# Six PSUM banks for the opening of layer 1, roundings one pair behind the tanh, and unread products around the attention of layer 0

## The chip, the cores and the metric

The kernel runs on one core of one Trainium2 chip. The metric is the device time of one execution in microseconds (us). A measurement of this kernel is the median of a few runs.

## The reference, cut to what matters

Two transformer layers over 1024 tokens of width 256. Each layer adds an attention and a feed-forward part, both computed from the same layer norm, to its input:

```python
x = L0_attn_X                                   # (1, 1024, 256)
xn = _layernorm(x)
x = x + _L0_attn_ref(xn, ...) + _L0_ffn_ref(xn, ...)   # 16 heads of 16, rope, causal; 1024 hidden, sign weights
xn = _layernorm(x)
x = x + _L1_attn_ref(xn, ...) + _L1_ffn_ref(xn, ...)   # 16 heads, 64+64 (rope) wide keys, 128 wide values
# _L1_ffn_ref: 32 experts of width 96, the best 4 for each token, and a shared expert:
sh = jax.nn.silu(x @ shared_gate_w.T) * (x @ shared_up_w.T)       # 512 hidden
shared_gate = jax.nn.sigmoid(x @ shared_expert_gate_w.T)
out0 = shared_gate * (sh @ shared_down_w.T)
```

## The kernel before, in words

Most products are made of three: each fp32 operand is split into a rounded part ("hi", copied to fp32r by ScalarE) and the rest ("lo", a subtraction on GpSimd or VectorE), and hi·hi, lo·hi and hi·lo are added in PSUM. PSUM is one tensor `bank` of eight banks of 512 fp32 columns. Each engine's program is written out by hand; semaphores order them. Between the blocks all engines meet.

**Block 1, `project_layer0`.** Layer norm, transposition, q, k and v of layer 0 with rope, then its feed-forward part. The last of TensorE's work is the down projection, 8 tiles of 16 products (line 453).

**Block 2, `attend_layer0`.** Eight pairs of heads. TensorE's order is a sorted list of steps that have a time in units of one pair. "max" steps (12 a pair, lines 680 and 662) make the scores of one row tile of both heads in one of two double banks; VectorE takes their row maxima (line 621). The "shift" step (line 691) transposes the maxima of the pair, which SyncE then writes as two more rows of q. "exp" steps (9 a pair, lines 708 and 659) make the transposed scores, shifted by these rows; ScalarE takes their exponentials (line 603). Pair p's max steps begin `LEAD` = 1.4 pairs ahead of its exp steps. "mix" steps (line 726) multiply the exponentials with v, into bank 7 (`O_BANK`); the first is at time 1.2. VectorE takes each finished half group out of bank 7 (line 638, semaphore `taken`). The score products have 48 or 50 contracted rows for each head, the mixes 32 columns of weights.

**Block 3, `join_layer0`.** Output projection (line 832), the sum, the second layer norm, transposition and the router's logits. Its first products wait until ScalarE has rounded `wo` (line 774) and VectorE has made the rest (line 798).

**Block 4, `layer1`.** It opens with the shared expert. TensorE's work is cut into units that each fill one bank; `unit_done` and `unit_free` count them. Units 0 to 7 are four pairs (gate, up), two for each of two slices of the hidden width; 8 to 15 are four q/k projections of head 0 (`qk_unit`) in turn with four output products (`out_unit`), the first of which waits for the lo part of all four pairs; 16 to 23 are four more pairs (5 to 8). Then come v of round 0 (four units from `V0_UNIT` = 24, line 1733), scores of the first rows and four more output products. All of them use banks 6 and 7 in turn (`unit_bank`), so unit n waits for `unit_free` ≥ n − 1. Banks 0 to 3 are for scores, 4 and 5 for transpositions.

For a pair, ScalarE takes the tanh of the gate half (line 1286), VectorE makes (tanh + 1)·gate (line 1361), multiplies by the up half (line 1365) and by the token's gate (line 1368), ScalarE rounds (`hidden_hi`, line 1259) and GpSimd makes the rest (`hidden_lo`, line 1614). Two buffers `hid`, which are the tanh's too, are used in turn. ScalarE's program for a pair is: tanh, one rounding of weights, `hidden_hi` of the same pair. Between the pairs VectorE also does the routing: softmax, the best four, weights, choice, and after the fifth pair (`HALF_UNIT[1]`) `route_place`, which yields the row of each token and expert in `slot_x`. Then GpSimd scatters the tokens (line 1638): four after the lo part of pair 6, four after that of pair 7, eight after that of pair 8, then it normalises the first rows of probabilities (line 1627), which the first transposition of the rounds (line 1824) waits for. After that come eight rounds of two heads, in which the experts' tiles are interleaved.

## Time and profile before

| | |
|---|---|
| times of three runs | 993.98, 996.51, 1004.88 us |
| median | 996.51 us |
| the profiled execution's own time | 1002.6 us |
| span of its profile | 1000.8 us |
| TensorE busy | 874.6 us, 87% |
| VectorE busy | 635.3 us, 63% |
| ScalarE busy | 421.8 us, 42% |
| GpSimd busy | 343.8 us, 34% |
| mean granted TensorE clock | 0.919 of 2.4 GHz |

The span leaves out 1.8 us of the execution's time. "Busy" counts a TensorE product from its start to its modelled end. The blocks meet at 80.4 us (layer-0 attention begins), 240.0 us (join) and 272.0 us (layer 1); the rounds' first transposition is at 359.5 us.

### The profile page before, as it was taken

How to read it: one execution, taken by the hardware profiler on the slowest of the kernel's cores; microseconds unless marked ns; L12 is line 12 of the kernel's file. 1: busy time of each engine (PE TensorE's matmuls, PEld its weight loads, DVE VectorE, ACT ScalarE, POOL GpSimd, SP SyncE). 2: the span in 40 equal slices, each digit the busy share in tenths (PEclk: the TensorE clock that was granted, in tenths of full speed). 3: DMA queues.
4: the chain of work that ended last, by engine and by line, in shares of the span. 5: the costliest groups of instructions: out<-in, count | busy, mean ns of one | idle time of the engine just before them, and what ended most of it. 6: DMA issues, size and time to landing. Idle time of an engine off the chain costs nothing.

```text
span 1000.8 us, 17106 instructions
## 1 busy us (share of the span) xinstructions
PE 874.6 (87%) x5280; PEld 605.1 (60%) x5280; DVE 635.3 (63%) x1179; ACT 421.8 (42%) x959; POOL 343.8 (34%) x333
## 2 busy tenths in 40 slices
PE   3697998886777777899999999999999999999665
PEld 2584544434555665576676676676767667667444
DVE  5697658753578546557656756756666666676552
ACT  3230546674322133435534625635535544543230
POOL 2340000001043675624423424324323433435780
PEclk9896559997878788999999999999999999999778
DMA  6550222420030111404413323422432331341221
GB/s 246 197 153 27 70 71 81 120 71 23 22 117 11 63 66 40 132 22 156 131 52 121 131 79 126 130 80 89 131 115 89 128 118 52 122 150 37 59 77 55
DMA packets 52773, 94.08 MB, mean 94 GB/s; under 512 B 6980, under 2 KB 27980, under 8 KB 52460
## 3 DMA queue, kind: packets, MB, share of 16 engines
q1 hardware_dynamic: 49660, 85.16, 26.7%
q0 software_dynamic: 3072, 8.39, 2.6%
q8 instruction: 24, 0.39, 0.2%
q14 instruction: 17, 0.14, 0.0%
HBM read 75.43 MB, written 24.78 MB: 100 GB/s over the span
## 4 chain that ended last, share of the span: by engine, by line
PE 48%; DVE 3%; issue 2%; POOL 2%; ACT 1%; POOLq 0%; DVEq 0%; ACTq 0%
PE bank L1841 10%; PE bank L1761 9%; PE bank L1711 7%; PE bank L1824 5%; PE bank L1751 4%; PE bank L1865 4%; PE bank L1733 3%; PE bank L1877 2%; PE bank L1858 1%; POOL d_gathered L1648 1%; DVE d_swap L1388 1%; PE bank L1764 1%; PE bank L1874 1%; DVE d_rot L1388 1%; PE bank L1749 0%
## 5 line engine op out<-in xcount | busy, mean ns | idle before, releaser
L1627 POOL TENSOR_SCALAR d_probs<-d_probs,d_row_inv 128x1024 f32<-128x1024 f32 (+7 forms) x128 | 99.3, 780 | 191.7 <-DVE d_row_inv L1416 190.8
L1268 ACT ACTIVATE d_probs<-bank,d_neg_max 128x1024 f32<-128x1024 f32 (+7 forms) x128 | 95.9, 753 | 104.4 <-DVE d_neg_max L1411 104.1
L1841 PE MATMUL bank<-d_pT,d_v 128*128 128x512 f32 (+3 forms) x384 | 130.9, 491 | 0.4 <-ACT d_pT L1315 0.4
L1411 DVE TENSOR_REDUCE d_neg_max<-bank 128x1 f32<-128x1024 f32 (+7 forms) x128 | 95.7, 753 | 51.4 <-PE bank L1764 50.7
L1315 ACT COPY d_pT<-bank 128x512 f32<-128x512 f32 x192 | 86.2, 488 | 80.2 <-PE bank L1824 80.2
L1841 PEld LDWEIGHTS bank<-d_pT,d_v 128*128 128x128 f32 x384 | 72.8, 192 | 59.6 <-issue 47.3
L621 DVE TENSOR_REDUCE b_maxes<-bank 128x2 f32<-128x1024 f32 (+2 forms) x96 | 89.0, 949 | 29.7 <-PE bank L662 20.1
L1824 PE MATMUL bank<-ident,d_probs 128*128 128x128 f32 x576 | 88.5, 285 | 15.3 <-POOL d_probs L1627 10.4
L1761 PE MATMUL bank<-d_k_hi,d_q_hi 128*128 128x512 f32 x192 | 78.3, 408 | 18.8 <-POOL d_k_lo L1621 14.2
L603 ACT ACTIVATE b_probsT<-bank 128x512 f32<-128x512 f32 x132 | 72.2, 594 | 48.3 <-PE bank L659 37.3
L1621 POOL TENSOR_TENSOR d_q_lo<-d_rot,d_q_hi 128x512 fp32r<-128x512 f32 x32 | 40.9, 1279 | 138.1 <-ACT d_q_hi L1264 138.1
L1824 PEld LDWEIGHTS bank<-ident,d_probs 128*128 128x128 f32 x576 | 66.8, 145 | 34.2 <-POOL d_probs L1627 12.9
L1761 PE MATMUL bank<-d_k_hi,d_q_lo 128*128 128x512 f32 x192 | 68.6, 358 | 0.0
L1761 PE MATMUL bank<-d_k_lo,d_q_hi 128*128 128x512 f32 x192 | 68.3, 356 | 0.0
L584 POOL TENSOR_TENSOR heads_lo<-acc,heads_hi 128x512 fp32r<-128x512 f32 x8 | 10.2, 1276 | 160.1 <-ACT heads_hi L609 160.1
L1711 PE MATMUL bank<-xT_hi,d_qkw_hi 128*128 128x512 f32 x128 | 57.5, 449 | 8.4 <-DVE d_slot_hT L1581 4.5
L1761 PEld LDWEIGHTS bank<-d_k_hi,d_q_hi 128*128 128x128 f32 x192 | 38.1, 199 | 38.1 <-issue 17.7
L1401 DVE TENSOR_TENSOR d_rot<-d_rot,d_swap 64x512 f32<-64x512 f32 x64 | 55.7, 871 | 6.7
L1564 DVE TENSOR_TENSOR d_head_lo<-bank,d_head_hi 128x512 fp32r<-128x512 f32 x32 | 22.1, 692 | 59.5 <-ACT d_head_hi L1323 59.3
L1388 DVE TENSOR_TENSOR d_swap<-bank,d_sin 32x512 f32<-32x512 f32 x64 | 44.4, 693 | 19.1 <-PE bank L1711 17.8
L1386 DVE SCALAR_TENSOR_TENSOR d_swap<-bank,d_gs_now,d_sin 32x512 f32<-32x512 f32 x64 | 48.2, 753 | 11.2 <-PE bank L1711 9.3
L1711 PE MATMUL bank<-xT_hi,d_qkw_lo 128*128 128x512 f32 x128 | 51.6, 404 | 0.0
(276 smaller groups left out, 2019.2 us busy)
## 6 DMA issues: line engine op xcount, KB each, us to landing
d_expert_w<-in_expert_w SPq DMA_DIRECT2D x102, 320.0 KB, 3.2
d_slot_x<-slot_x SPq DMA_DIRECT2D x51, 128.0 KB, 2.9
slot_y<-d_slot_y SPq DMA_DIRECT2D x49, 128.0 KB, 3.3
qk_raw<-in_w_qk SPq DMA_DIRECT2D x16, 256.0 KB, 3.3
slot_x<-in_zeros SPq DMA_DIRECT2D x5, 768.0 KB, 5.9
slot_x<-in_zeros SPq DMA_DIRECT2D x3, 896.0 KB, 6.4
d_vw_raw<-in_w_v SPq DMA_DIRECT2D x9, 256.0 KB, 3.2
q_stack<-a_part_hi SPq DMA_DIRECT2D x4, 512.0 KB, 5.1
```

The lines of the kernel that those rows point to most:

```text
L603: nc.scalar.activation(probs(head, n), bank[:, E_BANK + t % 3, :], ACT.Exp, scale=SCALE0).then_inc(exped, 1)
L621: nc.vector.tensor_reduce(maxes[:, p % 2, c, :, i], bank[:, first:first + 2, 0:w], AX_X, ALU.max, negate=True).then_inc(maxed, 1)
L1268: nc.scalar.activation(probs[s % NP_][:, 0:width(s)], score_bank(s, width(s)), ACT.Exp, bias=neg_max[:, h.col(s)], accum_out=row_sum[:, h. ...
L1315: nc.scalar.copy(pT[c][:, j:j + blocks, col:col + P], bank[:, T_BANK + tu % 2, 0:blocks * P].rearrange("p (b q) -> p b q", b=blocks)).then ...
L1388: return nc.vector.tensor_tensor(dst, src[rows, :], table[rows, cols], ALU.mult)
L1401: nc.vector.tensor_tensor(rot[n % 2][DS:P, :], rot[n % 2][DS:P, :], swap[DS:P, :], ALU.add).then_inc(rotated, 1)
L1411: nc.vector.tensor_reduce(neg_max[:, h.col(s)], score_bank(s, width(s)), AX_X, ALU.max, negate=True).then_inc(maxed, 1)
L1627: nc.gpsimd.tensor_scalar(probs[s % NP_][:, 0:width(s)], probs[s % NP_][:, 0:width(s)], row_inv[:, h.col(s)], 1.0, ALU.mult, ALU.mult).the ...
L1711: last = nc.tensor.matmul(out, parts(a, k), b[:, k, cols], start=(k == 0 and n == 0), stop=(k == KT - 1 and n == 2))
L1761: last = nc.tensor.matmul(out, a["q"][:, rows], b["k"][:, cols], start=(n == 0), stop=(n == 2 and not diagonal))
L1824: last = nc.tensor.transpose(bank[:, T_BANK + tu % 2, b * P:(b + 1) * P], probs[n % NP_][:, (j + b) * P:(j + b + 1) * P], ident[:])
L1841: last = nc.tensor.matmul(bank_of(h, "pv", n)[:, q:CH], v[:, j, h.hh, :], pT[c][:, j, q:CH], start=(j == 0), stop=(j == len(pieces) - 1))
```

## The change

Four edits.

1. In block 1 TensorE issues 14 products of 128x128 by 512 bf16 columns behind its last work, into bank 0. They and all below multiply the constants `halves`, and nothing reads their result.
2. In block 2 TensorE's list gets steps "keep", one such product each, into bank 7: 12 between the max steps of pair 0 (times from −1.36 to −0.48), and then one every 0.05 of a pair from −0.38 to 1.12, which are 31. When the last half group has been taken (`taken` = 8), 20 more follow.
3. Units 0 to 23 of layer 1 use banks 6, 7, 0, 1, 2 and 3 in turn (`wide_bank`), and unit n waits for `unit_free` ≥ n − 5. The first scores wait for `unit_free` ≥ 24, since they use banks 0 to 3. From `V0_UNIT` on the two banks stay.
4. ScalarE's and GpSimd's programs for pair p hold `hidden_hi` and `hidden_lo` of pair p − 1; those of the fourth and the eighth pair follow in the same step. The first eight scatters stand behind GpSimd's steps for the seventh and the eighth pair.

```diff
@@ project_layer0, TensorE
                 last.then_inc(down_done, 1)
+            for n in range(14):
+                nc.tensor.matmul(bank[:, 0, :], halves[:, 0, 0, :], halves[:].rearrange("p a f c -> p (a f c)"),
+                                 start=True, stop=True)
@@ attend_layer0
+    KEEP_UNITS, KEEP_STEP, AFTER = 12, 0.05, 20
+    def keep_steps():
+        first = [-LEAD + (n + 0.5) / RING for n in range(KEEP_UNITS)]
+        later = [1 - LEAD + 0.02 + KEEP_STEP * n for n in range(int((MIX_FROM + LEAD - 1 - 0.04) / KEEP_STEP))]
+        return [(at, "keep", 0) for at in first + later]
...
+            def keep_busy(n):
+                for _ in range(n):
+                    nc.tensor.matmul(bank[:, O_BANK, :], halves[:, 0, 0, :], halves[:].rearrange("p a f c -> p (a f c)"),
+                                     start=True, stop=True)
-            for name, at in ordered(max_steps(0) + shift_steps(-0.2) + exp_steps(0) + pieces):
-                if name == "max":
+            for name, at in ordered(max_steps(0) + shift_steps(-0.2) + exp_steps(0) + pieces + keep_steps()):
+                if name == "keep":
+                    keep_busy(1)
+                elif name == "max":
...
+            pe.wait_ge(taken, NG * NC)
+            keep_busy(AFTER)
@@ layer1
+    WIDE = (6, 7, 0, 1, 2, 3)
+    def wide_bank(unit):
+        return bank[:, WIDE[unit % len(WIDE)], :]
@@ layer1, ScalarE
-            for t in range(ST):
-                half = t // 2
-                for c in range(NC):
-                    p = t * NC + c
-                    act.wait_ge(unit_done, HALF_UNIT[half] + (t % 2) * 2 * NC + 2 * c + 1)
...
-                    hidden_hi(p, p % 2, t % 2, c, HALF_UNIT[half])
-                if t == 1:
+            for p in range(SHARED_PAIRS):
+                t, c, half = p // NC, p % NC, p // (2 * NC)
+                unit = HALF_UNIT[half] + 2 * (p % (2 * NC))
+                act.wait_ge(unit_done, unit + 1)
+                if p >= 2:
+                    act.wait_ge(hid_lo_done, p - 1)
+                nc.scalar.activation(tanh[p % 2][:], wide_bank(unit), ACT.Tanh, scale=0.5).then_inc(tanh_done, 1)
...
+                for q in ([p - 1] if p % (2 * NC) else []) + ([p] if p % (2 * NC) == 2 * NC - 1 else []):
+                    hidden_hi(q, q % 2, q // NC % 2, q % NC, HALF_UNIT[half])
+                if p == 2 * NC - 1:
                     for n in range(QK_UNITS):
                         qk_part_hi(0, n)
@@ layer1, GpSimd
+                for q in ([p - 1] if p % (2 * NC) else []) + ([p] if p % (2 * NC) == 2 * NC - 1 else []):
+                    hidden_lo(q, q % 2, q // NC % 2, q % NC)
...
+                if p in (SHARED_PAIRS - 2, SHARED_PAIRS - 1):
+                    for n in range(4):
+                        scatter((p - (SHARED_PAIRS - 2)) * 4 + n)
@@ layer1, TensorE
             def pair_units(unit, b, c):
                 for part in range(2):
-                    if unit is not None:
-                        pe.wait_ge(unit_free, unit + part - 1)
-                    project_T(unit_bank(part), lambda a, k: w_slice((gu_hi, gu_lo)[a][b], k, part), c)
+                    if unit + part >= len(WIDE):
+                        pe.wait_ge(unit_free, unit + part - (len(WIDE) - 1))
+                    project_T(wide_bank(unit + part), lambda a, k: w_slice((gu_hi, gu_lo)[a][b], k, part), c)
-                pe.wait_ge(unit_free, unit - 1)
+                pe.wait_ge(unit_free, unit - (ring - 1))          # qk_unit and out_unit, ring=6 here
...
                     v_unit(V0_UNIT, 0, unit_bank(0))
                     pe.wait_ge(qk_lo_done, 3)
+                    pe.wait_ge(unit_free, V0_UNIT)
                     scores(NT)
```

VectorE's steps for these units read `wide_bank` in place of `unit_bank`; their order is as before.

## Rows read from the trace of the kernel before

**Rows 1.** Page, the granted TensorE clock in 40 slices of 25 us, in tenths.

```profile
PEclk9896559997878788999999999999999999999778
```

**Rows 2.** Busy time by engine from one pair's shift step (L691) to the next; columns: window, length, PE, PEld, DVE, ACT, POOL, clock, DMA share, GB/s.

```profile
80.44:92.95 12.51, 7.28 (x56) 3.90 (x57) 11.02 (x13) 0.00 (x0) 0.00 (x0) 0.66 0.01 2
92.95:108.26 15.31, 13.40 (x94) 7.66 (x94) 11.65 (x14) 6.97 (x12) 0.00 (x0) 0.50 0.15 52
108.26:127.75 19.49, 19.02 (x137) 9.74 (x137) 11.84 (x14) 9.91 (x19) 0.00 (x0) 0.50 0.29 83
127.75:151.85 24.10, 23.61 (x163) 9.87 (x162) 13.33 (x18) 10.41 (x20) 1.27 (x1) 0.55 0.25 73
151.85:167.60 15.75, 13.56 (x162) 6.72 (x162) 12.83 (x18) 10.31 (x20) 1.28 (x1) 1.00 0.36 104
```

**Rows 3.** PE alone in windows of 2 us: PE busy, granted clock, DMA share, GB/s.

```profile
84.00:86.00 2.00, 1.21 (x10) 0.60 0.00 0
...
148.00:150.00 2.00, 1.74 (x12) 0.69 0.00 0
...
220.00:222.00 2.00, 1.31 (x22) 1.00 1.03 363
```

**Rows 4.** Timeline: the last work of block 1, block 2's first, two products of 512 columns.

```profile
78.86 0.28 PE L453 MATMUL bank<-a_down_sign,a_part_lo 128*128 128x256 f32 x1
79.64 0.48 DVE L383 SCALAR_TENSOR_TENSOR x<-token_x,a_outs,x 128x256 f32<-128x256 f32 x1
80.44 0.33 PE L680 MATMUL bank<-spare 48*128 48x128 f32 x2 [1.31 <-PEq L267]
...
279.23 0.39 PE L1711 MATMUL bank<-xT_hi,d_gu_hi 128*128 128x512 f32 x1
279.46 0.40 PE L1711 MATMUL bank<-xT_hi,d_gu_lo 128*128 128x512 f32 x1
```

**Rows 5.** Timeline from block 2's end to the join's start, and windows of all engines.

```profile
235.45 0.72 DVE L638 STREAM_TRANSPOSE acc<-bank 128x512 f32<-128x512 f32 x1 [7.47 <-PE bank L726]
239.98 1.04 ACT L774 CAST c_wo_hi<-wo 128x1024 fp32r<-128x1024 f32 x1 [1.67 <-PEq L557]
242.34 0.58 PE L832 MATMUL bank<-c_wo_hi,heads_hi 128*128 128x256 f32 x1 [6.95 <-DVE c_wo_lo L798]
...
32.00:34.00 2.00, 0.24 (x2) 0.00 (x0) 1.97 (x2) 0.00 (x0) 1.90 (x1) 1.00 0.00 0
238.00:240.00 2.00, 0.00 (x0) 0.00 (x0) 0.00 (x0) 0.34 (x2) 1.26 (x1) 0.50 0.00 0
242.00:248.00 6.00, 5.67 (x26) 5.67 (x27) 1.41 (x5) 1.32 (x2) 0.00 (x0) 0.50 0.22 66
```

**Rows 6.** VectorE, 277.9 to 327.7 us: groups (busy, mean ns, idle before), then timeline.

```profile
L1361 DVE SCALAR_TENSOR_TENSOR d_g_act<-d_hid,bank 128x512 f32<-128x512 f32 x5 | 3.4, 687 | 6.5 <-ACT d_hid L1286 6.5
L1365 DVE TENSOR_TENSOR d_g_act<-d_g_act,bank 128x512 f32<-128x512 f32 x5 | 3.4, 688 | 2.1 <-PE bank L1711 1.7
L1388 DVE TENSOR_TENSOR d_swap<-bank,d_sin 32x512 f32<-32x512 f32 x4 | 2.8, 693 | 1.8 <-PE bank L1711 1.8
...
277.96 0.69 DVE L1361 SCALAR_TENSOR_TENSOR d_g_act<-d_hid,bank 128x512 f32<-128x512 f32 x1 [5.00 <-ACT d_hid L1286]
279.43 0.69 DVE L1365 TENSOR_TENSOR d_g_act<-d_g_act,bank 128x512 f32<-128x512 f32 x1 [0.79 <-PE bank L1711]
283.60 1.21 DVE L1368 TENSOR_TENSOR d_hid<-d_g_act,d_cb 128x512 f32<-128x512 f32 x1
317.22 0.69 DVE L1361 SCALAR_TENSOR_TENSOR d_g_act<-d_hid,bank 128x512 f32<-128x512 f32 x1 [0.94 <-ACT d_hid L1286]
```

**Rows 7.** 327.7 us (route_place ends) to the rounds' first transposition: window, GpSimd group, timeline.

```profile
327.70:359.50 31.80, 24.31 (x111) 19.86 (x111) 14.81 (x22) 6.28 (x11) 24.04 (x24) 0.82 0.23 75
...
L1638 POOL DMA_INDIRECT slot_x<-token_x,d_x_row x16 | 16.3, 1016 | 4.5 <-issue 4.5
...
359.46 1.97 PE L1824 MATMUL bank<-ident,d_probs 128*128 128x128 f32 x8 [4.20 <-POOL d_expert_w L1679]
```

More of the change, by code:

```diff
@@ L146, in build @@
             with ExitStack() as b:
[L147 removed]
+                attend_layer0(nc, b, sb, bank, ident, halves, v_all, rope_scratch,
                               heads_hi, heads_lo, q_buf, k_buf,
@@ new lines, in _ @@
+            for p in range(SHARED_PAIRS):
[5 more added lines that the diff above has]
+                nc.scalar.activation(tanh[p % 2][:], wide_bank(unit), ACT.Tanh, scale=0.5).then_inc(tanh_done, 1)
+                if c == 0 and t + 1 < ST:
+                    gu_part_hi(t + 1)
+                elif t == 0:
+                    part_hi(qkw_hi[:], qk_raw[:], qk_in, 16, None, qkw_hi_done)
+                    act.wait_ge(gate_in, 16)
+                    nc.scalar.activation(ge[:], gl[:], ACT.Exp, scale=-1.0).then_inc(gate_step, 1)
+                elif c == 1 and t % 2 == 1:
+                    part_hi(ow_hi[:], ow_raw[:], ow_in, 16 * (half + 1), HALF_UNIT[half], ow_hi_done)
+                elif c == 1:
+                    part_hi(vw_hi[:], vw_raw[:], vw_in, 16, None, vw_hi_done)
+                for q in ([p - 1] if p % (2 * NC) else []) + ([p] if p % (2 * NC) == 2 * NC - 1 else []):
+                    hidden_hi(q, q % 2, q // NC % 2, q % NC, HALF_UNIT[half])
+                if p == 2 * NC - 1:
@@ L1360, in pair_steps @@
                 dve.wait_ge(hid_done, pair)
-                nc.vector.scalar_tensor_tensor(g_act[:], tanh[par][:], 1.0, unit_bank(0), ALU.add, ALU.mult
+                nc.vector.scalar_tensor_tensor(g_act[:], tanh[par][:], 1.0, wide_bank(unit), ALU.add, ALU.mult
                                                ).then_inc(unit_free, 1)
@@ L1364, in pair_steps @@
                 dve.wait_ge(unit_free, unit + 1)
-                nc.vector.tensor_tensor(g_act[:], g_act[:], unit_bank(1), ALU.mult).then_inc(unit_free, 1)
+                nc.vector.tensor_tensor(g_act[:], g_act[:], wide_bank(unit + 1), ALU.mult).then_inc(unit_free, 1)
                 dve.wait_ge(unit_free, unit + 2)
@@ L1532, in _ @@
                     for n in range(QK_UNITS):
-                        rope(QK0_UNIT + 2 * n, 0, n, unit_bank(0), first=True)
-                        out_add(QK0_UNIT + 2 * n + 1, n, unit_bank(1))
+                        rope(QK0_UNIT + 2 * n, 0, n, wide_bank(QK0_UNIT + 2 * n), first=True)
+                        out_add(QK0_UNIT + 2 * n + 1, n, wide_bank(QK0_UNIT + 2 * n + 1))
                 else:
@@ L1656, in _ @@
             gu_part_lo(0)
[L1657 to L1671 removed]
+            for p in range(SHARED_PAIRS):
+                t, c = p // NC, p % NC
+                if c == 0 and t + 1 < ST:
+                    gu_part_lo(t + 1)
+                elif t == 0:
+                    part_lo(qkw_lo[:], qk_raw[:], qkw_hi[:], qkw_hi_done, 1, qkw_lo_done)
+                elif c == 1 and t % 2 == 1:
+                    part_lo(ow_lo[:], ow_raw[:], ow_hi[:], ow_hi_done, t // 2 + 1, ow_lo_done)
+                elif c == 1:
+                    part_lo(vw_lo[:], vw_raw[:], vw_hi[:], vw_hi_done, 1, vw_lo_done)
+                for q in ([p - 1] if p % (2 * NC) else []) + ([p] if p % (2 * NC) == 2 * NC - 1 else []):
+                    hidden_lo(q, q % 2, q // NC % 2, q % NC)
+                if p == 2 * NC - 1:
                     for n in range(QK_UNITS):
                         qk_part_lo(0, n)
+                if p in (SHARED_PAIRS - 2, SHARED_PAIRS - 1):
+                    for n in range(4):
+                        scatter((p - (SHARED_PAIRS - 2)) * 4 + n)
             for n in range(8, PREFACE_SCATTERS):
@@ L1736, in v_unit, with out_unit @@
                 last.then_inc(unit_done, 1)
-            def out_unit(unit, n, out, products, add_experts=False):
+            def out_unit(unit, n, out, products, add_experts=False, ring=2):
                 k, c = n // NC, PV_CHUNK[n % NC]
-                pe.wait_ge(unit_free, unit - 1)
+                pe.wait_ge(unit_free, unit - (ring - 1))
                 rows, cols = slice(k * P, (k + 1) * P), slice(c * CH, (c + 1) * CH)
@@ L1783, in _ @@
                         unit = HALF_UNIT[a] + (t % 2) * 2 * NC + 2 * c
-                        pair_units(unit if unit else None, SHARED_BUF[t], c)
+                        pair_units(unit, SHARED_BUF[t], c)
                 output = [(b, hid_hi[:, b, :], hid_lo[:, b, :]) for b in range(2)]
```

39 lines of the change are left out of this document (6 added, 33 removed).

## Prediction

> **What bounds the kernel now.** I first read the granted clock in the page's slices [rows 1]: it is near its upper level (2.4 GHz) almost everywhere, and at half (1.2 GHz) in slices 5 and 6 of 40, which is the first half of layer 0's attention. The chain that ended last says why the clock matters: in the rounds of layer 1, from some 440 us on, it is TensorE without a gap. No edit touches the rounds, so the change is decided before 360 us, and I read two stretches there.
>
> The first is layer 0's attention, by pairs [rows 2]. At the upper level a pair takes 15.75 us, with VectorE busy for 12.83 and TensorE for 13.56: both nearly full. At the half level the pairs take 15.31, 19.49 and 24.10 us, and TensorE is busy for 13.40, 19.02 and 23.61 of them: there TensorE bounds. The reader should see when the clock fell and when it came back [rows 3]: it fell within 84 to 86 us, in the thin stretch behind the block's start, and rose only within 148 to 150 us, 64 us later, though TensorE was nearly always busy in between. At the end of the same block it stayed 1.00 at a busy share like that at which it had fallen (1.31 of 2.00 us in 220 to 222, 1.21 in 84 to 86). So the share of busy time doesn't tell by itself what the clock will do, which is the main risk here.
>
> The second is the opening of layer 1. There the order of waits is VectorE until `route_place` ends at 327.7 us, then GpSimd. In the 31.80 us from there to the first transposition of the rounds GpSimd is busy for 24.04 us and loses 4.5 us in issue between its 16 scatters [rows 7]; the rest is the fifth-to-sixth pair's path ahead of the first scatter. TensorE then waits 4.20 us for the last of GpSimd's work [rows 7]. So what counts is how early `route_place` ends.
>
> **Edit 1, 14 products ahead of the attention.** The last product of block 1 starts at 78.86 us, block 2's first at 80.44 [rows 4]. The nearest row for the price of one product is the distance of two with 512 columns at the upper level: 279.46 − 279.23 = 0.23 us [rows 4]. 14 of them are 3.3 us and end at about 82.4; VectorE's tail of block 1 ends at 79.64 + 0.48 = 80.12 us and block 2 begins 0.3 us later [rows 4], so it would begin at 82.7, which costs 2.3 us. Nothing hides it but that tail. Bounds: 1.7 us (0.20 us each) to 3.3 us. The Trainium skill ("TensorE: Matmul & The Clock Gate", Back-to-back issue gap) gives 512 columns some 216 ns at the upper clock; by that, as an estimate, edit 1 would cost 2.0 us.
>
> **Edit 2, 43 products within the attention, if the clock stays up.** I take the four steps to the shift of pair 3 one by one, which took 12.51 + 15.31 + 19.49 + 24.10 = 71.4 us [rows 2].
> - Pair 0's maxima: VectorE is busy 11.02 of 12.51 us [rows 2] and sets the pace already. One product of 0.23 us for each of 12 units goes into TensorE's gaps (it is busy 7.28 of 12.51). I take 12.1 us; 12.0 to 12.5.
> - Next: VectorE needs 11.65 us. TensorE's 13.40 us at half become 7.7 us (by the ratio of 13.56 to 23.61, pairs with the same work [rows 2]); 20 added products are 4.7 us, together 12.4 us, under the pace. In the steady pair 15.75 − 12.83 = 2.9 us of VectorE are waits. 11.65 + 2.4 gives 14.0 us, since there is no taking out yet and half of the exp steps are missing; 12.7 to 15.75.
> - Next: 11.84 + 2.9 = 14.7 us. TensorE: 19.02 × 0.57 = 10.9 and 11 products for 2.6 us, 13.5 us, as in the steady pair. 13.3 to 15.75.
> - Next: the steady 15.75 us.
>
> Together 56.6 us, and 58.9 with edit 1, against 71.4: **12.5 us won**; bounds 8.6 (both middle steps at the steady pace, edit 1 at 3.3 and pair 0 at 12.5) and 15.6 us. The later four pairs don't change.
>
> **The 20 products behind the attention.** They start when the last half group is taken, at 236.2 us (235.45 + 0.72 [rows 5]), and end 20 × 0.23 = 4.6 us later, so that the meeting moves from 240.0 to 241.4 us: 1.4 us lost, for ScalarE's rounding of `wo`, which the join waits for, starts with the block. What they may give back is the join's slow start: 26 products in 5.67 us at clock 0.50 [rows 5] would take half, 2.8 us less. But TensorE still idles for some 2.7 us between the last of them and the first product of the join (242.34 − 239.98 = 2.4 us behind the meeting [rows 5]). In the trace an idle time like this has gone both ways: with TensorE idle in 32 to 34 us it stayed 1.00, and after the idle from 235.4 on the clock was 0.50 in 238 to 240 [rows 5]. Ends: 1.4 us lost and 1.4 us won. I take 0, between them.
>
> **Edits 3 and 4, layer 1.** VectorE's waits from the first pair to `route_place` are: for the tanh 6.5 − 5.0 = 1.5 us, for up units 1.7, for q/k units 1.8 [rows 6]. Of these stays the 0.79 us for the very first up unit (its products follow the first tanh at the half clock, whatever the banks), and most of the 0.94 us ahead of the fifth pair [rows 6]: the tanh stands behind the roundings of the ropes in ScalarE's queue, the last of which needs VectorE's last rope, so some 0.5 us is left. With six banks TensorE is units ahead everywhere else. Won: 5.0 − 0.8 − 0.5 = **3.7 us**. New waits: `hidden_lo` of a pair now stands behind a rounding of weights on GpSimd, and the tanh two pairs on waits for it; VectorE has a routing function between any two of the first pairs, and of its 49.8 us here no wait for GpSimd is among the groups [rows 6], which is the cover; without it a wait would be one GpSimd step, 16.3 / 16 = 1.0 us or a little more by its scatters' row [rows 7]. The first output product then waits on TensorE until the lo part of the fourth pair, about 1 us sooner than before, and VectorE's choice and gates, which stand between the fourth pair and the first rope, cover it; TensorE had no wait there that VectorE felt before the second rope. The new wait ahead of the first scores holds TensorE's v units and output products, but all of these end well ahead of GpSimd's scatters. Behind `route_place` GpSimd has the same work in another order (four scatters ahead of the lo parts of pairs 7 and 8, twelve behind), so its 31.8 us stay, and the output products, some 5 us sooner, only lengthen TensorE's wait. What could cost: one multiplication of two SBUF operands took 1.21 us and not 0.69 beside a GpSimd subtraction (283.60 [rows 6]); four such meetings would take 2.1 of the 3.7 us. Ends: 1.6 us, and 4.5 us if the fifth pair's wait goes too.
> The Trainium skill ("SBUF — State Buffer", the rules on the shared port pair) says that a VectorE instruction with two SBUF inputs contends with a GpSimd instruction that reads SBUF, and one of them is blocked meanwhile. This row agrees; by that rule the later subtractions can hit any of the pairs' last multiplications, and the gain would be the lower end, 1.6 us.
>
> **Sum.** 12.5 + 0 + 3.7 = 16.2 us. From the profiled execution's 1002.6 us this gives 986.4. That execution is 6.1 us above the median of 996.51. From the median the same sum gives 980.3. If the 6 us lie in the stretch at half clock, which came back at a chance moment, the change takes them away too, and 986 is the time; if they lie elsewhere, 980. The forecast is the middle, **983 us**.
>
> **Rivals.**
> - *The clock holds, the opening of layer 1 gives nothing* (a new wait or shared-port blocking takes 3.7 us): 987 us. For it: VectorE's margins there are under 1 us. Against: of the waits in [rows 6] only the two named depend on something else than banks and the order of ScalarE.
> - *The clock falls during pair 0 all the same, and comes back with the added products before the mixes begin.* Then pair 0 takes 12.5 us and the next step 13.40 + 10 × 0.47 (ten products at the half clock) = 18 us, the rest as forecast: 4.4 us lost, 987 to 991 us. For it: TensorE's idle time in pair 0, 12.51 − 7.28 = 5.2 us [rows 2], is only half filled by 12 × 0.23 = 2.8 us.
> - *Slower: the products don't count for the clock.* They multiply mostly zeros, at K = 128, and come one at a time. If the clock is at half from about 85 us to the mixes, every added product costs 0.47 us on an engine that is full: TensorE 13.40 + 9.3 = 22.7 us for the second step (7.4 more), 19.02 + 5.1 = 24.1 for the third (4.7 more), 2.3 us at the start, 1.4 us at the end, less 3.7 us: 12 us slower, 1009 us. It decides where the clock is under 0.9 from pair 0's shift on. Against it: at the upper level it has held at 1.31 of 2.00 us busy [rows 3], and the added products bring pair 0 from 0.58 (7.28 of 12.51) to over that. The Trainium skill ("TensorE: Matmul & The Clock Gate", Part 1) says that throttled is the default state and that activity releases it. The trace disagrees in part: TensorE was busy 19.02 of 19.49 us and stayed at 0.50 [rows 2]; by the rule alone the clock would have been back without this edit.
>
> **How the numbers follow.** Within 1% (about 10 us) a measurement of this kernel can't tell from no change. The forecast has 0.60, layer 1 without gain 0.12, the late return 0.13, slower 0.12, and 0.03 is left for anything else. The forecast's own bounds are 8.6 − 1.4 + 1.6 = 8.8 and 15.6 + 1.4 + 4.5 = 21.5 us won, on a start between 996.5 and 1002.6; I keep 974 to 990. The range goes up to 998 to take in the second and third cases and leaves out the slow one: 974 to 998. Faster by over 1% is below 986.5 us: most of the forecast, a third of the next two, 0.64. Slower by over 1%, 0.12. The same, 0.24.
>
> **What would show it.** Clock 1.00 in every window from 80 to 150 us; shift steps (L691) at about 94.8, 108.8, 123.5 and 139.3 us and then every 15.75; block 2's first product at 82.7. TensorE's products in the join at 0.12 us distance if its clock held. In layer 1 no wait of VectorE for L1711 apart from the first, and `route_place` ending 46.0 us behind the first pair's first VectorE step, 3.7 us less than now; GpSimd without gaps from there to L1824, 31.8 us. Wrong would be: a clock of 0.50 behind 85 us, a pair step of 20 us or more, a new wait of VectorE for ACT or POOL in the pairs.

## The result and the profile after

The changed kernel takes **1016.52 us** (median of 4 runs, 1012.05 to 1021.03) against 996.38 us of the kernel before on the same chip: ratio 1.0183, 95% interval [1.0132, 1.0234]. It is slower. The forecast was 983 us, range 974 to 998. Ratios, here and below, leave out executions that took over 1.5% longer than the fastest of their kernel; medians leave out none. The profiled execution took 1018.45 us, its span is 1016.7 us against 1000.8 before.

I read the new profile in the order of the forecast: the clock first. Two lines of the page's 40 slices (25.4 us each), tenths of busy time of TensorE and of its granted clock:

```profile
PE   3698998989777567899999999999999999999666
PEclk9897559997987778899999999999999999999878
```

Slices 5 and 6 still read 5, as before [rows 1]: the stretch at half clock has not gone. Next the steps of layer 0's attention, from the block's start to the shift of pair 0, then to the shifts of pairs 1, 2, 3 and 4, then two windows near the block's end. Columns: length of the window, busy us of each engine (instructions), granted clock, DMA share, GB/s.

```profile
core 0: us, PE busy (x) PEld busy (x) DVE busy (x) ACT busy (x) POOL busy (x), PEclk, DMA share, GB/s
83.34:96.74 13.40, 11.16 (x68) 4.72 (x69) 11.29 (x13) 0.00 (x0) 0.00 (x0) 0.77 0.01 2
96.74:120.65 23.91, 23.10 (x112) 9.52 (x114) 11.97 (x14) 6.96 (x12) 0.00 (x0) 0.50 0.10 34
120.65:146.88 26.23, 25.27 (x148) 10.80 (x148) 11.96 (x14) 9.90 (x19) 0.00 (x0) 0.50 0.21 62
146.88:164.71 17.83, 16.79 (x163) 7.24 (x162) 13.23 (x18) 10.41 (x20) 1.27 (x1) 0.86 0.33 98
164.71:180.43 15.72, 13.53 (x162) 6.71 (x162) 12.83 (x18) 10.31 (x20) 1.28 (x1) 1.00 0.37 104
234.00:240.00 6.00, 5.32 (x42) 2.13 (x40) 0.71 (x1) 3.20 (x7) 0.00 (x0) 0.50 0.30 105
240.00:248.00 8.00, 7.79 (x44) 2.07 (x40) 2.11 (x4) 3.81 (x8) 1.28 (x1) 0.52 0.00 0
```

Against [rows 2]: 0.9 us more in pair 0, 8.6 in the second step, 6.7 in the third, 6.3 less in the fourth, where the clock came back sooner within the step. VectorE's work is nearly unchanged; TensorE's busy time in the second and third steps rose from 13.40 to 23.10 and from 19.02 to 25.27 us, and the steps followed it. The windows around the fall and the return, of the same view, same columns:

```profile
84.00:88.00 4.00, 3.67 (x31) 1.85 (x31) 3.57 (x5) 0.00 (x0) 0.00 (x0) 1.00 0.02 6
88.00:90.00 2.00, 1.36 (x10) 0.68 (x10) 1.74 (x3) 0.00 (x0) 0.00 (x0) 1.00 0.00 0
90.00:92.00 2.00, 1.73 (x6) 0.57 (x5) 1.81 (x3) 0.00 (x0) 0.00 (x0) 0.65 0.00 0
...
148.00:152.00 4.00, 4.00 (x30) 1.33 (x22) 3.03 (x6) 1.60 (x4) 0.00 (x0) 0.50 0.02 4
152.00:156.00 4.00, 3.73 (x50) 1.88 (x46) 2.94 (x4) 2.67 (x5) 0.29 (x1) 0.99 0.27 67
```

The 14 and the first products of pair 0 put the fall off by some 6 us, from 85 [rows 3] to 91 us (3 of the 6 are the later start of the block); they did not prevent it. What one added product cost is in the groups of their lines: ahead of the block (upper level), and between 93 and 127 us (lower level). Columns: busy us, mean ns of one, idle time before.

```profile
L458 PE MATMUL bank<-halves 128*128 128x512 bf16 x13 | 3.0, 379 | 0.1
```

```profile
L681 PE MATMUL bank<-halves 128*128 128x512 bf16 x25 | 14.5, 613 | 0.3 <-issue 0.3
```

At the upper level 13 take 3.0 us, 0.23 us each, as forecast. At the lower one 25, which stand among small products, take 14.5 us of TensorE: 0.58 us each.

**The whole account, profiled execution against profiled execution.** Block 2 begins 2.9 us later (83.34 against 80.44; 0.9 of it is in block 1 ahead of the 14 products, which are 2.0). The attention takes 176.4 against 159.5 us: 16.9 more, of which 10.0 in the four steps above and 6.9 between the last shift and the block's end, where the clock was at 0.50 from 234 to 247 us. The join takes 28.8 against 32.1 us: 3.2 less. Layer 1 up to the end of `route_place` takes 54.0 against 55.5, from there to the first transposition 31.4 against 31.9: 2.0 less together. The rest is 1.3 us longer. 2.9 + 16.9 − 3.2 − 2.0 + 1.3 = 15.9 us, the difference of the spans. The medians differ by 20.1 us, because the profiled execution of before lies 6.2 us above its median and this one 1.9 above.

The join behind the 20 products, TensorE in the order of time (start, us, line, what it waited for); before it was 26 products in 5.67 us [rows 5]:

```profile
262.10 0.39 PE L853 MATMUL bank<-c_wo_hi,heads_hi 128*128 128x256 f32 x1 [2.63 <-DVE c_wo_lo L819]
262.32 0.28 PE L853 MATMUL bank<-c_wo_hi,heads_lo 128*128 128x256 f32 x1
262.44 0.28 PE L853 MATMUL bank<-c_wo_lo,heads_hi 128*128 128x256 f32 x1
```

The distance of the next two is 0.12 us, and the granted clock over the whole join (259.74 to 288.56 us) is 1.00: it held through an idle time of 2.63 us.

In layer 1, VectorE's instructions with a wait, and those that took much longer than before:

```profile
294.48 0.69 DVE L1389 SCALAR_TENSOR_TENSOR d_g_act<-d_hid,bank 128x512 f32<-128x512 f32 x1 [4.99 <-ACT d_hid L1313]
295.92 0.69 DVE L1393 TENSOR_TENSOR d_g_act<-d_g_act,bank 128x512 f32<-128x512 f32 x1 [0.76 <-PE bank L1740]
299.91 1.67 DVE L1396 TENSOR_TENSOR d_hid<-d_g_act,d_cb 128x512 f32<-128x512 f32 x1
306.24 1.19 DVE L1492 TENSOR_SCALAR d_probs<-d_probs 128x8 f32<-128x8 f32 x1
307.71 0.97 DVE L1495 SCALAR_TENSOR_TENSOR d_top_w<-d_probs 128x32 f32<-128x32 f32 x1
332.22 0.69 DVE L1389 SCALAR_TENSOR_TENSOR d_g_act<-d_hid,bank 128x512 f32<-128x512 f32 x1 [0.47 <-ACT d_hid L1313]
```

The other waits are gone as forecast [rows 6], but a step on eight columns now takes over a microsecond.

### The profile page after: what moved, and what is told of

The parts are those of the page before. It is cut to its first block, busy times and chain, and to the rows that moved or that the text cites. A ratio compares the mean times of both kernels' runs of the same rounds, so it can differ in the third digit from the quotient of the medians.

```text
span 1016.7 us, 17253 instructions
## 1 busy us (share of the span) xinstructions
PE 895.2 (88%) x5350; PEld 608.3 (60%) x5357; DVE 637.6 (63%) x1179; ACT 421.3 (41%) x959; POOL 342.5 (34%) x333
## 4 chain that ended last, share of the span: by engine, by line
PE 48%; DVE 3%; issue 2%; POOL 1%; ACT 1%; POOLq 0%; DVEq 0%; ACTq 0%
PE bank L1871 10%; PE bank L1790 9%; PE bank L1740 7%; PE bank L1854 5%; PE bank L1780 4%; PE bank L1895 4%; PE bank L1762 3%; PE bank L1907 2%; PE bank L1888 1%; DVE d_swap L1416 1%; PE bank L1793 1%; POOL d_gathered L1676 1%; PE bank L1904 1%; DVE d_rot L1416 1%; PE bank L1778 0%
## 5 line engine op out<-in xcount | busy, mean ns | idle before, releaser
L1871 PE MATMUL bank<-d_pT,d_v 128*128 128x512 f32 (+3 forms) x384 | 133.1, 497 | 0.4 <-ACT d_pT L1343 0.4
L1740 PE MATMUL bank<-xT_lo,d_qkw_hi 128*128 128x512 f32 x128 | 51.8, 405 | 0.0
```

The costliest lines, as they stand in the source:

```text
L1740: last = nc.tensor.matmul(out, parts(a, k), b[:, k, cols], start=(k == 0 and n == 0), stop=(k == KT - 1 and n == 2))
L1871: last = nc.tensor.matmul(bank_of(h, "pv", n)[:, q:CH], v[:, j, h.hh, :], pT[c][:, j, q:CH], start=(j == 0), stop=(j == len(pieces) - 1))
```

## The experiments

Theory A: with the clock at half, each added product lengthens a TensorE that is already full; the kernel is slow because the clock fell, and what lets it fall is how few products stand in pair 0. Rival B: the products' data (mostly zeros) is what doesn't hold the clock. Rival C: the layer-1 edits cost part of it. All ratios are to the kernel before on the same chip, with 95% intervals.

**1. Layer 1 alone, products alone, the 20 alone.** `e1_layer1_only` is before with edits 3 and 4:

```diff
-            for n in range(14): ...               # block 1
-  ... + pieces + keep_steps()):
+  ... + pieces):
-            keep_busy(AFTER)
```

> Edits 3 and 4 alone (six banks, roundings one pair behind), no added product. In the changed kernel's profile the stretch from the start of layer 1 to the end of route_place took 54.1 us, against 55.7 us before, and the rounds kept their pace. Theory (the added products carry the whole loss): this kernel is 1 to 2 us faster than the kernel before, with that stretch near 54 us and VectorE's multiplications of two SBUF operands up to 1.2 to 1.7 us beside GpSimd's subtractions. Rival (layer 1's edits lose time in some other way, since later waits moved): 2 us or more slower than before.

Measured: 1000.07 us (991.58 to 1004.12), ratio 1.0011 [0.9970, 1.0052]; layer 1 to the end of `route_place` 54.0 us, to the first transposition 85.4 against 87.4.

`e2_products_only` is the changed kernel with edits 3 and 4 taken back:

```diff
-    WIDE = (6, 7, 0, 1, 2, 3)
...
-                for q in ([p - 1] if p % (2 * NC) else []) + ...:
-                    hidden_hi(q, q % 2, q // NC % 2, q % NC, HALF_UNIT[half])
+                    hidden_hi(p, p % 2, t % 2, c, HALF_UNIT[half])
```

> Edits 1 and 2 alone (77 added products), layer 1 as before. Theory: the loss of 16 to 20 us is here. The granted clock falls to 0.50 at about 90 us in spite of the products, and from there to about 150 us each of them costs 0.54 us of a full TensorE: the second and third pair step take 23 and 26 us, the attention block is some 13 to 17 us longer, the join 3 us shorter, and the kernel is 12 to 20 us slower than before. Rival (the two halves of the change spoil each other, for example by the phase of the clock): less than 8 us slower.

Measured: 1019.53 us, ratio 1.0196 [1.0114, 1.0277]. The loss is in the products, and `e1_layer1_only` shows none; rival C falls.

`e3_behind_only` is before with only `keep_busy(AFTER)` behind the attention.

```diff
+            pe.wait_ge(taken, NG * NC)
+            keep_busy(20)
```

> Of all edits only the 20 products behind the attention. Theory: the clock is held for the join, whose time goes from 32.1 us to some 29, and the meeting comes 1.0 to 1.5 us later: 1.5 to 2.5 us faster than before. Rival (the clock falls all the same in the idle time behind them): 1.4 us slower. The clock in the attention is 0.50 from about 84 us on, as before.

Measured: 995.81 us, ratio 0.9989 [0.9954, 1.0024]. From the last shift to the block's end 26.03 us against 25.03: 1.0 us lost. The join took 31.0 us against 32.1; in this execution its clock was 0.89, in the changed kernel's 1.00. The gain of 1.5 to 2.5 us that I had expected does not show in the medians.

**2. More products in pair 0, or other data.** `e5_dense` puts three at each of pair 0's 12 places, `e4_two_a_unit` two:

```diff
-        first = [-LEAD + (n + 0.5) / RING for n in range(KEEP_UNITS)]
+        first = [-LEAD + (n + 0.5) / RING for n in range(KEEP_UNITS) for _ in range(3)]
```

> The changed kernel with three added products ahead of each of pair 0's max steps in place of one (36 and not 12); all else as changed. Theory (the clock fell at 90 us because TensorE still had thin moments between max steps, at 88.0 to 89.0 us only 0.36 of 1 us busy): pair 0 takes some 16 us and not 13, the clock stays 1.00 through it and through the later steps, which take 14 to 16 us each: the attention block is 8 to 12 us shorter than before the change and the kernel 6 to 12 us faster than before. Rival (these products don't count for the clock, whatever their number, since they multiply mostly zeros): the clock is 0.50 from about 90 us on and the kernel is another 5 us or more slower than the changed one, over 20 us slower than before.

> The changed kernel with two added products ahead of each of pair 0's max steps (24), between the changed kernel's one (clock fell at 90 us) and three (clock 1.00 throughout, mean 0.955 of the execution, pair 0 took 14.9 us). Theory (the clock is held if TensorE has no thin moments): pair 0 takes some 13.5 us; if two are enough, the clock is 1.00 to 150 us and the kernel is 1 to 2 us faster than the one with three, 993 to 995 us; if not, it falls between 84 and 98 us and the kernel takes over 1010 us, with executions on either side likely. Rival (only the number of added products in pair 0 matters little, and luck decided): the same spread as with three, some executions falling.

Measured: 995.71 us, 0.9983 [0.9949, 1.0018], and 994.69 us, 0.9979 [0.9945, 1.0013]. Both profiles hold the clock at 1.00 through all steps in which it had fallen, and nine of the ten executions of either have a mean clock of 0.950 to 0.956; the tenth took 1014.14 and 1017.40 us at 0.930 and 0.927. `e5_dense` by steps (columns as above):

```profile
83.39:98.57 15.18, 14.08 (x91) 5.66 (x93) 11.49 (x13) 0.00 (x0) 0.00 (x0) 1.00 0.01 2
98.57:113.08 14.51, 13.76 (x111) 6.47 (x113) 11.68 (x14) 6.96 (x12) 0.00 (x0) 1.00 0.17 56
113.08:129.38 16.30, 15.04 (x148) 7.27 (x149) 11.59 (x14) 9.90 (x19) 0.00 (x0) 1.00 0.34 100
```

Twelve more products than the change has (`e4_two_a_unit`) bring some 20 us back. But the time is that of before, no better, where I had expected 6 to 12 us less of `e5_dense`.

`e6_real_data` keeps the change's counts and places and multiplies fp32 values of v instead (128 columns, also unread):

```diff
-                    nc.tensor.matmul(bank[:, O_BANK, :], halves[:, 0, 0, :], halves[:].rearrange("p a f c -> p (a f c)"),
-                                     start=True, stop=True)
+                    nc.tensor.matmul(bank[:, O_BANK, 0:P], v_all[:, 0, 0:4, :].rearrange("p h e -> p (h e)"),
+                                     v_all[:, 1, 0:4, :].rearrange("p h e -> p (h e)"), start=True, stop=True)
```

> The changed kernel with its counts and places of the added products, but each multiplies real fp32 data (128x128 by 128 columns of v, at about the price in time of 512 bf16 columns) and not the mostly zero constants. Rival (the products didn't count because of their zeros): the clock is held at 1.00 through the attention, mean clock about 0.95, and the kernel takes 988 to 996 us. Theory (their number and places were the reason, not their operands): the clock falls between 84 and 98 us as in the changed kernel, mean clock 0.92 to 0.93, and the kernel takes 1010 to 1020 us.

Measured: 1021.18 us, ratio 1.0235 [1.0163, 1.0306]; the clock fell at about 100 us. Rival B falls as the cause: zeros in greater number held the clock, and real data in the same places did not. Type and shape changed with the data here, and in this one profile the clock stayed 1.00 for 14 us of the block, not 7; whether the data helps a little is not shown.

**3. Which of the products are needed.** `e7_pair0_only`: 36 in pair 0, none of the 31 later. `e8_no_lead_in`: 36 and 31, without the 14. `e9_thin_later`: 24 in pair 0, 15 later.

```diff
+        first = [... for n in range(KEEP_UNITS) for _ in range(3)]      # e7 and e8; range(2) in e9
-        return [(at, "keep", 0) for at in first + later]
+        return [(at, "keep", 0) for at in first]            # e7
-            for n in range(14): ...                         # e8
-    KEEP_UNITS, KEEP_STEP, AFTER = 12, 0.05, 20
+    KEEP_UNITS, KEEP_STEP, AFTER = 12, 0.1, 20              # e9
```

> The kernel with three products a unit in pair 0, without the 31 products behind pair 0 (those that the changed kernel puts at every 0.05 of a pair). Theory (thin moments let the clock fall; the pair steps are denser than pair 0 by their exp steps): the clock stays 1.00; the second and third step take 13 to 14 and 14 to 15 us in place of 14.6 and 16.3, so the kernel is 2 to 3 us faster than with them, 992 to 994 us. Rival (the 31 products are needed, since at half clock the same steps never raised the clock): the clock falls behind 98 us and the kernel takes 998 to 1003 us, as if pair 0's products were lost.

> The kernel with three products a unit in pair 0, without the 14 products behind block 1. Theory (block 1 ends dense and the clock falls only after several thin microseconds, so the products in pair 0 do the holding): block 2 begins 2 us earlier, the clock stays 1.00 and the kernel is 2 us faster than with them, some 993.5 us. Rival (the lead-in is needed to bridge the meeting of the engines): clock 0.50 from about 85 us on, and with 67 products at half clock over 1010 us.

> The changed kernel with two products at each of pair 0's 12 max units (24) and one every 0.1 of a pair behind that (15) in place of one every 0.05 (31). If the products of pair 0 decide the clock, it stays 1.00 through the attention as with 24 + 31, and the second and third step are shorter by 16 products of 0.23 us or less: 14.0 and 15.3 us in place of 14.5 and 16.3, and the median is about 1.5 us under that of 24 + 31 (994.7). If the later products are needed as well, the clock falls in the second or third pair, those steps take 19 us or more, and the median is 998 to 1004.

Measured: e7 998.23 us, 1.0004 [0.9969, 1.0039]; e8 996.69 us, 1.0009 [0.9962, 1.0055]; e9 1006.35 us, 1.0059 [1.0019, 1.0099], which I had expected to win. Of e9, pair 0 and what follows, and of e7 its second and fourth step:

```profile
82.72:92.00 9.28, 9.06 (x65) 3.66 (x66) 7.49 (x9) 0.00 (x0) 0.00 (x0) 1.00 0.01 3
92.00:96.00 4.00, 2.93 (x21) 0.99 (x17) 3.63 (x5) 0.00 (x0) 0.00 (x0) 1.00 0.00 0
96.00:100.00 4.00, 3.75 (x29) 1.89 (x30) 3.12 (x5) 1.54 (x2) 0.00 (x0) 0.79 0.02 3
100.00:112.00 12.00, 11.44 (x70) 5.84 (x70) 7.34 (x9) 5.25 (x10) 0.00 (x0) 0.50 0.20 67
...
100.25:115.16 14.91, 12.68 (x93) 7.25 (x94) 11.49 (x14) 6.97 (x12) 0.00 (x0) 0.55 0.17 55
134.78:160.28 25.50, 25.14 (x163) 10.27 (x161) 13.42 (x18) 10.41 (x20) 1.27 (x1) 0.50 0.24 69
```

In both the clock held in pair 0 and fell in the second step (in e7 at 102 us, until 177), so the later products are needed as well as pair 0's. This profile of e7 is of its slowest execution, 1015.85 us at a mean clock of 0.917; the other ten took 995.41 to 1000.24 us at 0.940 to 0.945, between before and the kernels that held it, and have no trace. In e8 every window of 4 us from 80 to 152 us is at 1.00, so the 14 are not needed; seven of its ten executions are at 0.950 to 0.953 and three at 0.933 to 0.938, which took 1006 to 1008 us. In the profiled one of these three the clock fell at 152 us in a steady pair, far from any added product, which ran at 1.00 in the profile of before:

```profile
148.00:152.00 4.00, 3.50 (x58) 2.31 (x60) 3.90 (x6) 2.60 (x5) 0.00 (x0) 1.00 0.57 129
152.00:156.00 4.00, 3.98 (x30) 1.61 (x30) 3.46 (x6) 1.35 (x4) 0.00 (x0) 0.52 0.84 269
```

`e11_later_only` has the 31 later products without the 14 and the 12:

```diff
-            for n in range(14): ...
-        return [(at, "keep", 0) for at in first + later]
+        return [(at, "keep", 0) for at in later]
```

> The changed kernel without the 14 and without the 12 in pair 0: the 31 later products and all else stay. By the theory that the later products cost 0.54 us each on a full TensorE once the clock is at half, and that nothing in pair 0 holds it up here, the clock is 0.50 from about 85 us on, the second and third step take 23 and 26 us as in the changed kernel, and the median is 1010 to 1018. By the rival that only the lead-in and pair 0's single products let the clock fall (they end in a thin stretch), the clock falls as in before and the 31 bring it back earlier: third step under 20 us, median 995 to 1000.

Measured: 1015.29 us, ratio 1.0136 [1.0087, 1.0185]. Its steps:

```profile
81.49:93.99 12.50, 7.77 (x57) 4.17 (x57) 11.02 (x13) 0.00 (x0) 0.00 (x0) 0.60 0.01 2
93.99:117.89 23.90, 23.10 (x111) 9.52 (x114) 11.96 (x14) 6.97 (x12) 0.00 (x0) 0.50 0.10 34
117.89:144.12 26.23, 25.27 (x147) 10.81 (x147) 11.96 (x14) 9.91 (x19) 0.00 (x0) 0.50 0.21 62
```

The second and third steps are those of the changed kernel to 0.1 us, so the price of the 31 at half clock is isolated: with the 31 products TensorE is busy for 48.37 us in the two steps, against 32.42 in before [rows 2]: some 16 us more, 0.51 us each, and they did not bring the clock back.

**4. The two layer-1 edits apart.** `e12_banks_only` is before with the six banks alone; `e10_behind_and_layer1` has both layer-1 edits and the 20. The cut shows what e12 takes back of edit 4; none of the added products is in it either.

```diff
-                for q in ([p - 1] if p % (2 * NC) else []) + ([p] if p % (2 * NC) == 2 * NC - 1 else []):
+                for q in [p]:                               # e12, on ScalarE and GpSimd
-                if p in (SHARED_PAIRS - 2, SHARED_PAIRS - 1):
+                if p in (SHARED_PAIRS - 3, SHARED_PAIRS - 2):
```

> Before with six banks for units 0 to 23 of layer 1, and nothing else: roundings and the first scatters stay in their old places. If the banks are what shortens the opening, the stage from layer 1's start to the end of route_place takes 54.0 us as with both layer-1 edits (55.5 before), and the waits for up units (L1365 in before) are gone but those for the tanh stay (6 us in all with q/k less), so the gain may be half of it: 54.0 to 54.8 us. If the roundings' order is the one that counts, the stage is 55.2 to 55.5 us. The median is within 2 us of before either way.

> The changed kernel without the 14 and the 43 products: the 20 behind the attention and the layer-1 edits stay. If the stages add up (join 1 us shorter by the profile with the 20 alone, opening of layer 1 up to the first transposition 2 us shorter by the profile with the layer-1 edits alone), the median is 2 to 3 us under before, 993 to 995. If the layer-1 gain of 2 us in the traces was only a difference between executions, the median is 996, as with the 20 alone.

Measured: e12 **993.42 us**, ratio 0.9955 [0.9919, 0.9992]; e10 995.92 us, 0.9994 [0.9955, 1.0034]. The stage to the end of `route_place` took 52.9 us in e12 and 54.0 in both kernels with the new order. So the banks win 2.7 us there, more than the 0.7 to 1.5 that I had expected of them, and the order of the roundings loses 1.1. VectorE's busy time in the stage says where, first `e12_banks_only`, then `e1_layer1_only`:

```profile
264.59:317.44 52.85, 40.75 (x153) 31.57 (x153) 43.54 (x101) 12.85 (x24) 21.39 (x20) 0.84 0.21 71
```

```profile
268.47:322.46 53.99, 39.99 (x153) 31.05 (x153) 45.25 (x101) 13.53 (x25) 21.69 (x20) 0.84 0.22 69
```

The same 101 instructions are 1.7 us longer; before they took 42.96 us. VectorE's idle time in the stage is 0.6 us less with the new order, hence the 1.1. Three small routing steps are 2.8 us longer (the two below, and one on 128x16 with 1.12 for 0.10 us), while steps on 128x32 in `route_place`, which had paid in the old order, are 1.2 us shorter. Both engines of `e1_layer1_only` around two of them, in the order of time:

```profile
286.02 1.26 POOL L1616 TENSOR_TENSOR d_ow_lo<-d_ow_raw,d_ow_hi 128x512 fp32r<-128x512 f32 x1 [1.27 <-ACT d_ow_hi L1261]
286.13 1.19 DVE L1471 TENSOR_SCALAR d_probs<-d_probs 128x8 f32<-128x8 f32 x1
287.24 1.26 POOL L1621 TENSOR_TENSOR d_hid_lo<-d_hid,d_hid_hi 128x512 fp32r<-128x512 f32 x1
...
287.59 0.96 DVE L1474 SCALAR_TENSOR_TENSOR d_top_w<-d_probs 128x32 f32<-128x32 f32 x1
```

and the same two lines in `e12_banks_only`, where one subtraction ends at 280.65 and the next starts at 282.53, behind the start of both:

```profile
282.04 0.17 DVE L1471 TENSOR_SCALAR d_probs<-d_probs 128x8 f32<-128x8 f32 x1
282.48 0.19 DVE L1474 SCALAR_TENSOR_TENSOR d_top_w<-d_probs 128x32 f32<-128x32 f32 x1
```

The subtractions often come in twos in either order; in the new one they stand where the small routing steps are, and a step of 0.17 us that starts beside one ends with it. The Trainium skill ("SBUF — State Buffer", Who interferes with whom) names both kinds: an instruction with two SBUF inputs, as L1474, and a `tensor_scalar` in a two-port mode, which L1471 may be, contend with a GpSimd instruction that reads SBUF. Both rows agree; in the prediction I had taken up only the first kind.

**5. Combinations.** `e13_banks_and_behind` adds the 20 to the six banks; `e14_banks_and_two` has the six banks, two products at each place of pair 0, the 14, the 31 and the 20, and the old order of roundings.

```diff
+                for q in [p]:                               # both, as e12
+            keep_busy(AFTER)                                # e13
+        first = [... for n in range(KEEP_UNITS) for _ in range(2)]   # e14, with the 14 and the 31
```

> Before with six banks for units 0 to 23 and the 20 products behind the attention; roundings in their old places. If the order of the roundings costs what the traces say, the stage from layer 1's start to the end of route_place is 52.9 us, as with the banks alone, against 54.0 with both layer-1 edits. If the 20 products are worth the 1 to 1.8 us that the join was shorter with them, the median is 992; if the clock of the join comes out even over many executions, it is 993.4, as with the banks alone.

> The changed kernel with two products at each max unit of pair 0 (24 + 31, and the 14 and the 20), but with the roundings and the first scatters in their old places. By the theory that terms add: 994.7 of the same with edit 4, less 1.2 us, 993.5, and the stage to the end of route_place 52.9 us. A held clock is then worth nothing against the banks alone (993.4), because the products cost what it gives. The rival, that edit 4's cost in the trace is chance: stage 54 us and 994.7.

Measured: e13 993.06 us, 0.9972 [0.9935, 1.0008]; e14 993.99 us, 0.9949 [0.9920, 0.9978]. Two of e14's twelve executions took 1010.12 and 1014.90 us at a mean clock of 0.93, the others 989.40 to 996.40 at 0.949 to 0.959. The stage to the end of `route_place` was 53.0 us in both, against 54.0 with the new order, so the price of the new order came out once more. The forecast's four steps in e14, and below them the stretch from the last shift to the block's end:

```profile
85.37:98.38 13.01, 11.73 (x79) 4.48 (x81) 11.11 (x13) 0.00 (x0) 0.00 (x0) 1.00 0.01 2
98.38:112.90 14.52, 13.73 (x111) 6.47 (x114) 11.68 (x14) 6.97 (x12) 0.00 (x0) 1.00 0.16 56
112.90:129.20 16.30, 14.71 (x147) 7.25 (x149) 11.58 (x14) 9.91 (x19) 0.00 (x0) 1.00 0.34 100
129.20:145.02 15.82, 14.66 (x162) 6.53 (x162) 13.04 (x18) 10.42 (x20) 1.28 (x1) 1.00 0.37 111
...
208.10:238.69 30.59, 26.18 (x216) 9.76 (x217) 6.60 (x13) 15.81 (x30) 3.82 (x3) 0.83 0.09 32
```

and in `e12_banks_only`, which has none of the products:

```profile
81.36:93.86 12.50, 7.76 (x56) 4.16 (x57) 11.02 (x13) 0.00 (x0) 0.00 (x0) 0.60 0.01 2
93.86:109.17 15.31, 13.40 (x93) 7.65 (x93) 11.65 (x14) 6.96 (x12) 0.00 (x0) 0.50 0.15 52
109.17:128.66 19.49, 18.93 (x138) 9.68 (x138) 11.84 (x14) 9.90 (x19) 0.00 (x0) 0.51 0.28 83
128.66:144.47 15.81, 14.66 (x162) 6.54 (x162) 13.04 (x18) 10.41 (x20) 1.27 (x1) 1.00 0.39 112
...
207.55:232.59 25.04, 17.80 (x197) 6.78 (x197) 6.60 (x13) 15.68 (x31) 3.82 (x3) 0.96 0.11 38
```

59.6 us at full clock against 63.1 with the clock at half for 44 us: 3.5 us, less 2 for the 14 products. By the steps the held clock is worth about 1.5 us. Two pairs of kernels differ in just the 14, the 24 and the 31 products: `e14_banks_and_two` and `e13_banks_and_behind` (0.9949 and 0.9972, 2.3 us), and `e4_two_a_unit` and `e10_behind_and_layer1` (0.9979 and 0.9994, 1.5 us). Both fit, and neither difference is clear of the intervals. Nor does a clock that is held through these steps stay up: in this profile of e14 it was at half again from 215 to 225 us, and the stretch from the last shift took 30.6 us against 25.0, of which one is the 20 products; in `e4_two_a_unit` it was so from 215 to 222 us.

## Why the prediction was wrong, point by point

- **The step that failed** is the condition of edit 2, "if the clock stays up". I argued that pair 0 would be busier than the stretch of 1.31 of 2.00 us at which the clock had once held. It was (5.03 of the 6.00 us from 84 to 90, still at 1.00), and the clock fell all the same at 91 us and stayed at half for 61 us. The rival "slower: the products don't count for the clock" is what happened in effect, at a chance of 0.12. Its reason was only half right: zeros do count (e4 and e5 held with them); one at each place was too few.
- **That rival's price** was 12 us; the profile shows 15.9. Its second step was forecast 7.4 us longer and was 8.6, its third 4.7 and was 6.7: TensorE rose by 9.7 us for 20 products in the second, 0.49 us each, and by 6.3 for 11 in the third, 0.57 each, where I took 0.47. The clock's return in the fourth step gave 6.3 back, and a second fall at 234 us took about 5.9, both not in my sum. Against the medians the loss is 20.1 us: an execution of before that is typical seems to have its clock back sooner than the profiled one (next point).
- **What a held clock is worth** was oversized by far: 12.5 us forecast, about 1.5 measured. So 983 us would have been too low with the clock held, too: e4, which held it and has both layer-1 edits, took 994.69 us. Two errors. First, the four steps took 71.4 us only in the profiled execution. The other five profiles without products within the attention took 63.1 (e3, e10, e12) and 65.6 us (e1, e13). I had written "if the 6 us lie in the stretch at half clock"; as far as these profiles show they did, and I used them for where the end lies and not for the gain, which against 63.1 us and my 56.6 shrinks to 6.5 us, less 2 for edit 1. The later runs show how often: of 25 executions of before on one chip 17 took 992 to 998 us at a mean clock of 0.927 to 0.936, and eight over 1002 us at 0.911 to 0.921, and the profiled one, with 0.919, is of the second kind. Second, at full clock the steps took 13.0, 14.5, 16.3 and 15.8, together 59.6 (e14), not 56.6: the third was forecast 14.7 and took 16.3, with TensorE busy 14.7 to 15.0 us in place of my 13.5. The ratio 0.57 holds: the fourth step, which has no added product, kept TensorE busy for 25.14 us at 0.50 (e7) and 14.66 at 1.00 (e12), 0.58. By it the third step's own work is 11.1 us, which leaves 3.6 for the eleven products, 0.33 each; the second step leaves 5.9 for 20, 0.30. What failed is the price of 0.23, read from products back to back and used for products among small ones. The waits of the third step were undersized, too: 16.3 − 11.6 = 4.7 us beside VectorE's work, forecast 2.9.
- **Edit 1**: 2.0 us measured, 2.3 forecast. The estimate in the prediction from the figure of the Trainium skill ("TensorE: Matmul & The Clock Gate", Back-to-back issue gap), 2.0, was the nearer one. The trace agrees: 13 products took 2.97 us, and without the last one's own 0.38 us their starts are 0.216 us apart.
- **The 20 products**: 1.0 us lost against 1.4. What they give back depends on the clock: the join was 3.2 us shorter where it held throughout, 1.1 in e3, 1.7 to 1.8 in e10, e13 and e14. I took 0 in all; it is 0 to 2 us won, and no median shows it.
- **Edits 3 and 4**: forecast 3.7 us to the end of `route_place`, measured 1.5 there and 2.0 with what follows. The waits went as listed: 0.76 for the first up unit stayed (0.79 forecast), 0.47 at the fifth pair (0.5). The mis-sized term is the one that I named and did not put into the sum: steps held up by GpSimd. I looked for it at the multiplications of the pairs; it also came at routing steps of eight columns. The lower bound, 1.6 us, which the prediction also gave by the rule of the Trainium skill ("SBUF — State Buffer", Who interferes with whom), was the nearer value. With the banks alone it is 2.7 + 0.4 = 3.1 us.
- **Behind `route_place`**: 31.8 us forecast to stay, 31.4 measured.
- **Slips in the bounds**: the terms named for edit 2 give 8.4 and 16.0 us, not 8.6 and 15.6, and the upper end of edits 3 and 4 is 5.0 − 0.8 = 4.2, not 4.5. They change nothing in the outcome.

Open: why the clock returned at about 128 us in some executions and at 149 in others, with TensorE busy for nearly all of the two steps ahead of it in both; why it fell at 152 us in e8, and why it falls later in the attention in kernels with and without products there (e10 and e8 at 152 us, e1 and e13 at 217 to 219, e14 and e4 at 215). No busy share in a row tells these apart, and I have no mechanism for it. What is shown is the effect of number and places in these kernels, not what the clock reacts to.

## What to carry to other kernels

Filler products are a bet with an uneven stake: while the clock is up much of their cost hides in idle time, and when it falls all the same each one costs about 0.5 us on an engine that is now the bound. Here the stake was 20 us and the prize about 1.5. Before a stretch at half clock is priced, look at it in more than one execution, and price it by the step that the other engine would then set. And free a wait by more banks rather than by a new order, where another order makes two engines meet in SBUF.

## What the runs showed of the hardware

- The clock fell and stayed at 0.50 with TensorE busy nearly all the time: in e9 it fell within 96 to 100 us, behind 13.3 us of which TensorE was busy for 12.0, in e8 at 152 us behind 4 us with 3.50 busy. The level then lasted some 31 us in e8, 44 in e12, 61 in the changed kernel, 72 in e11 and 75 in e7.
- It held through 2.63 us without any product behind the 20 fillers, and through the join's thin stretches (21.27 of 28.82 us busy at 1.00).
- A product of 512 bf16 columns takes 0.23 us at the upper level back to back (13 in 3.0 us). Among small products it takes more: 0.30 to 0.37 us at the upper level (in e14 23 in 7.0 us and 9 in 3.3), and 0.49 to 0.58 us at the lower.
- A VectorE step on 128x8 elements took 1.19 us beside a GpSimd subtraction of 1.26 us, and 0.17 us without it.
